# Keeping split weights in memory between the halves of a fused attention and expert kernel, with a reordered prologue and scattered expert rows

## The reference, cut to what matters

```python
xn = _layernorm(x)                                   # 4 x 512 x 512
x = x + attn(xn) + ffn(xn)
...
q, k, v = xn @ Wq.T, xn @ Wk.T, xn @ Wv.T            # 32, 8, 8 heads of 128; rope on q and k
dt = softplus(xn @ Win.T + dt_bias)
g = dt * -exp(A_log_bias)
G = cumsum(g)                                        # within a chunk of 128 tokens
y_intra = (q k^T * causal exp(G_i - G_j)) @ (v * dt)
y_inter = (q * exp(G)) @ state                       # state carried over 4 chunks
y = rmsnorm(y_intra + y_inter) * gnorm_w
attn = (y * silu(xn @ Wg.T)) @ Wo.T
...
scores = softmax(xn @ router_w + router_b) + router_bias
idx = top 2 of 16 experts, out of the best 2 of 4 groups
ffn = sum over the 2 picks of score * expert(xn) + shared_expert(xn)
```

## Time and profile before

| | us |
|---|---|
| median of 3 runs | 2282.23 (2272.57 to 2285.56) |
| the profiled execution | 2264.45 |
| its span in the trace | 2262.7 |
| PE busy | 2073.3 (92% of the span) |
| DVE busy | 1827.1 (81%) |
| ACT busy | 1396.9 (62%) |
| POOL busy | 1012.8 (45%) |

### The profile page before, as it was taken

One profiled execution on the slowest core, in us unless ns is written; L12 is line 12 of the kernel. 1 busy time (PEld: TensorE's weight loads), 2 busy tenths in 40 slices (PEclk: granted clock), 3 DMA queues, 4 the chain that ended last, 5 costly groups with the idle time before them and its releaser, 6 DMA issues.

```text
span 2262.7 us, 34001 instructions
## 1 busy us (share of the span) xinstructions
PE 2073.3 (92%) x9564; PEld 1619.0 (72%) x9564; DVE 1827.1 (81%) x3418; ACT 1396.9 (62%) x2722; POOL 1012.8 (45%) x810
## 2 busy tenths in 40 slices
PE   4699999999999999998899999999999999999990
PEld 2477777777777777776677777777777777767770
DVE  4788888888888888867888888888888888758884
ACT  5366666666666666652566666666666666637870
POOL 1234454545454545444354545454545454432215
PEclk9899999999999999999899999999999999999995
DMA  7212121212121212135121212121212121228667
GB/s 253 72 38 67 37 66 37 65 37 65 37 65 37 65 37 65 37 89 172 38 56 38 65 37 65 37 65 37 65 37 65 37 65 37 75 87 307 212 210 242
DMA packets 150876, 182.26 MB, mean 81 GB/s; under 512 B 13191, under 2 KB 89575, under 8 KB 150782
## 3 DMA queue, kind: packets, MB, share of 16 engines
q1 hardware_dynamic: 135006, 147.08, 22.5%
q0 software_dynamic: 7424, 21.00, 3.0%
q10 hardware_dynamic: 8352, 13.17, 1.6%
HBM read 152.88 MB, written 28.33 MB: 80 GB/s over the span
## 4 chain that ended last, share of the span: by engine, by line
PE 74%; DVE 7%; issue 7%; POOL 6%; ACT 3%; DMA 2%; DVEq 0%; SPq 0%; POOLq 0%; ACTq 0%
PE PJ L1216 10%; PE PJ L1218 10%; PE PJ L1217 10%; PE OU L1216 5%; PE OU L1218 5%; PE OU L1217 5%; PE TR L1360 4%; PE YE L1218 2%; PE YE L1217 2%; PE YE L1216 2%; PE SC L1216 2%; PE CS L1216 2%; PE CS L1217 2%; PE CS L1218 2%; PE YI L1216 2%
## 5 line engine op out<-in xcount | busy, mean ns | idle before, releaser
L444 POOL TENSOR_TENSOR zl<-yb,zh 128x512 fp32r<-128x512 f32 x122 | 162.5, 1332 | 318.4 <-ACT zh L942 318.2
L1216 PE MATMUL OU<-woh,zh 128*128 128x512 f32 x488 | 229.9, 471 | 18.1 <-POOL wol L693 10.2
L1710 DVE TENSOR_TENSOR t<-PJ,cosb 128x512 f32<-128x512 f32 x160 | 110.2, 688 | 168.6 <-PE PJ L1218 120.9
L1216 PE MATMUL PJ<-xnh,wqh 128*128 128x512 f32 x544 | 225.4, 414 | 10.6 <-DVE t L1712 5.8
L958 ACT ACTIVATE qh<-t 128x512 fp32r<-128x512 f32 x128 | 80.9, 632 | 224.0 <-DVE t L1715 224.0
L1218 PE MATMUL PJ<-xnh,wql 128*128 128x512 f32 x544 | 214.4, 394 | 0.0
L1217 PE MATMUL PJ<-xnl,wqh 128*128 128x512 f32 x544 | 214.0, 393 | 0.0
L1216 PE MATMUL PJ<-xnh,wgh 128*128 128x512 f32 x512 | 206.4, 403 | 2.4 <-POOL wgl L693 1.7
L723 POOL TENSOR_TENSOR gm<-gbc,amask 128x512 f32<-128x512 f32 x128 | 166.7, 1303 | 85.2 <-DMA gbc<-decay_exponents 57.4
L1218 PE MATMUL PJ<-xnh,wgl 128*128 128x512 f32 x512 | 201.5, 393 | 0.0
L1217 PE MATMUL PJ<-xnl,wgh 128*128 128x512 f32 x512 | 200.9, 392 | 0.0
(11 more groups left out here) (506 smaller groups left out, 6306.9 us busy)
## 6 DMA issues: line engine op xcount, KB each, us to landing
gbc<-decay_exponents SPq DMA_DIRECT2D x128, 256.0 KB, 4.8
stage<-in_wq SPq DMA_DIRECT2D x72, 256.0 KB
stage<-in_wg SPq DMA_DIRECT2D x64, 256.0 KB
stage<-in_wo SPq DMA_DIRECT2D x64, 256.0 KB
gbc<-in_wm SPq DMA_DIRECT2D x48, 256.0 KB
expert_rows<-rs ACTq DMA_DIRECT2D x48, 256.0 KB
stage<-in_wkv SPq DMA_DIRECT2D x34, 256.0 KB
experts<-in_wm SPq DMA_DIRECT2D x16, 512.0 KB, 6.3
```

The source lines that it names most:

```text
L444: nc.gpsimd.tensor_tensor(lo[:], yb[:, c, :], hi[:].bitcast(F32), ALU.subtract).then_inc(S["zlo"], 1)
L1216: nc.tensor.matmul(out_, a_hi, b_hi, start=first, stop=False)
L1710: v.tensor_tensor(t1[:], PJ[bank][:], cosb[:], ALU.mult)
```

## The change

In half 0, SP also writes both parts of every split piece to memory (`wsp`, shown as `split_weights`). Half 1 loads the two parts straight into their tiles and splits nothing but its first `wq` and the shared expert's weights. The layer norm has smaller groups and six ring buffers, and the decay chain is done by half (256 columns at a time): half 0's before the ropes, half 1's between them. In the middle, the first `wq` is free sooner, and the ranks are made one chunk earlier. In the experts, the map of slots holds beside each token the row where the result belongs, POOL scatters each tile's result there, and at the end SP loads 16 contiguous pieces of 512 KB.

The core of the diff:

```diff
-LN_GROUPS = [slice(0, 2), slice(2, 4), slice(4, 8), slice(8, 16)]
+LN_GROUPS = [slice(0, 2), slice(2, 4), slice(4, 6), slice(6, 8), slice(8, 12), slice(12, 16)]
...
-        xring = [t2[:, 0, :], t2[:, 1, :], gbc[:, 0, :], gbc[:, 1, :]]
+        xring = [t2[:, 0, :], t2[:, 1, :], gbc[:, 0, :], gbc[:, 1, :], st[:], y2[:]]
...
+                    def store_split(k, j):
+                        hold(sp, wsp_out[j % 2], wsp_out_from + 32 * (k * 7 + j // 2))
+                        for i, part_ in enumerate(split_place(j)):
+                            dst = wsp[bass.ds(split_row(k, j), 1), j, i].rearrange("o p n -> (o p) n")
+                            sp.dma_start(dst, plain(part_)).then_inc(wsp_out[j % 2], 16)
+
                     def att_piece(j, src):
                         piece(half, (6 + kv * 14 + j, j % 2), src)
 
+                        if j >= 2:
+                            store_split(kv, j - 2)
...
+                    def load_split(j, back):
+                        for i, part_ in enumerate(split_place(j)):
+                            src = wsp[bass.ds(split_row(kv, j), 1), j, i].rearrange("o p n -> (o p) n")
+                            sp.dma_start(plain(part_), src).then_inc(back, 16)
...
+                    elif half == 1:
+                        gload(0)
+                        gload(1)
+                        at.before("oproj", 4)
...
+                        for j in range(4, 8):
+                            load_split(j, wo_back)
+                        gload(2)
+                        at.wait("proj", 6)
+                        for j in (8, 9):
+                            load_split(j, wkv_back)
+                        gload(3)
+                        for j in range(10, 14):
+                            load_split(j, wq_back)
...
                     def w_lo(j, hi_out, lo_out):
-                        split_lo(half, (6 + kv * 14 + j, j % 2), hi_out, lo_out)
+                        if half == 0:
+                            split_lo(half, (6 + kv * 14 + j, j % 2), hi_out, lo_out)
...
                         def w_hi(j, hi_out):
+                            if half == 1:
+                                return
+                            if not (type(kv) is int and kv == 0):
+                                act.wait_ge(wsp_out[j % 2], wsp_out_from + 32 * (j // 2 - 6) + kv * 224)
                             split_hi(half, (6 + kv * 14 + j, j % 2), hi_out)
...
+            def scatter_rows(i):
+                pool.wait_ge(m_ev, i + 1)
+                g.indirect_dma_start(osd, bass.IndirectOffsetOnAxis(ap=idxt[:, i, 1:2], axis=0), mo[i % 4],
+                                     None).then_inc(mo_out[i % 4], 16)
+
+            for i in range(MT):
+                if i + 4 < MT:
+                    gather_x(i + 4)
+                if i:
+                    scatter_rows(i - 1)
+            scatter_rows(MT - 1)
...
-            act.wait_ge(u_down, NT)
+            act.wait_ge(wq_free, 1)
...
+            results = osd[0:NTA * PICKS * P, :].rearrange("(t p k) n -> t p (k n)", p=P, k=PICKS)
+            for t in range(NTA):
+                sp.dma_start(experts[:, t, :], results[t]).then_inc(pk_in[t // 2][0], 16)
```

More of the change, by code:

```diff
@@ L438, in shared_base, with shared_piece, split_place, split_row @@
         def shared_base(half):
-            return piece_base(half) + 6 + 14 * KV
+            return piece_base(half) + shared_piece(half)
+        def shared_piece(half):
+            return (6 + 14 * KV, 6)[half]
+        def split_place(j):
+            if j < 4:
+                return wgh[:, j, :], wgl[:, j, :]
+            if j < 8:
+                return woh[:, j - 4, :], wol[:, j - 4, :]
+            if j < 10:
+                return wkvflat(wkvh, j - 8), wkvflat(wkvl, j - 8)
+            return wqh[:, j - 10, :], wql[:, j - 10, :]
+        def split_row(kv, j):
+            return kv if j < 8 else kv + 1
         def z_lo(pool, at, c, hi=zh, lo=zl):
@@ L578, in shared_pieces @@
                 for i in range(4):
-                    piece(half, (6 + 14 * KV + i, i % 2), ws1[:, i * PW:(i + 1) * PW])
+                    piece(half, (shared_piece(half) + i, i % 2), ws1[:, i * PW:(i + 1) * PW])
+                    if half == 0 and i < 2:
+                        hold(sp, wsp_out[i], wsp_out_from + 32 * (7 * KV - 1))
+                        for k, part_ in enumerate(split_place(12 + i)):
+                            sp.dma_start(wsp[KV, 12 + i, k], plain(part_)).then_inc(wsp_out[i], 16)
             def shared_bias(half):
@@ L870, in _ @@
             act.wait_ge(const_made, CONSTS)
+            a.activation(klf[:, 511:512], one[:, 0:1], ACT.Sqrt)
             def deviation(r):
@@ L1081, in step @@
                                 silu_gate(c + 1)
+                                if c == 1 and first and half == 0:
+                                    act.wait_ge(g_out, 16 * 8)
                                 exp_g(c + 1)
@@ L1371, in step @@
                             weights(0)
+                        if first and half == 0:
+                            sum_decays(0)
                         at.wait("roperd", 1)
@@ L1379, in step @@
                         ins.then_inc(S["tr"], 1)
+                        if first and half == 0:
+                            turn_decays(0)
                         proj_q(1)
@@ L1389, in step @@
                             proj_q(j)
-                            if j == 2 and first and half == 0:
-                                sum_decays()
                         if b == 1:
@@ L1403, in step @@
                         proj_g(0)
+                        if first and half == 0:
+                            turn_decays(1)
                         at.wait("ropelo", 4)
@@ L1770, in step @@
                             v_rows()
+                            if first:
+                                route_ranks()
                             rope(1, 0)
```

489 lines of the change are left out of this document (277 added, 212 removed).

## The result

| | before | changed |
|---|---|---|
| median of 20 runs, us | 2274.0 | 2263.89 |
| lowest and highest, us | 2260.98, 2285.56 | 2249.14, 2270.24 |
| span of the profiled execution, us | 2262.7 | 2250.4 |

The ratio is 0.9944, with a 95% interval of 0.9924 to 0.9965; the medians differ by 10 us, where 56 were forecast.

A forecast was written before the change was run, and what follows sets the result against it. PE was taken to bound the kernel (busy 2073.3 of 2262.7 us), leaving 189 us of its idle time. Terms −22 (layer norm, step 0) + 2 − 9 − 16 + 0 − 11 = −56 us gave 2226 against the median, range 2196 to 2260.

The forecast's parts named there:

- Half 1, steady: Half 1's later steps: without weight subtractions POOL is 3 us earlier, PE's wait vanishes, 1.0 us over 16 steps: −16 us.
- late loads: Rival: half 1's loads come 2 us late each step, turning the 16 us gain into a loss; 2258 us, chance 0.05.
- The one of the stores: Rival: half 0's stores cost PE about 2.5 us per step, giving back 36 us; 2262 us, chance 0.12.
- the second rival: Half 1 gains nothing because DVE's own ropes set the scores; net −40 us, 2242 us, chance 0.10.
- Half 0: Half 0's steady steps: the added stores cost +2 us over seven groups, bounds −4 and +10.
- Step 0: First step of half 0: shorter waits for the decay chain and scores' inputs, −14.5 us, bounds −7 and −19.
- the layer norm: Start of the kernel: smaller groups and two more ring buffers remove three waits, −7.5 us, between −3 and −16.
- The middle: Between the halves: waits for `wql`, `wgl` and `zl` lose their cause, −9 us, between −4 and −14.
- The experts: Expert loop: tiles stay at 3.71 us with a gather and a scatter each, 0 us, between −4 and +12.
- the end: After the last expert tile: contiguous loads at 309 GB/s, 44 us instead of 55.7, −11 us, between −4 and −15.
- the 2.17 that would decide: Rival: POOL becomes the experts' bound, deciding once a scatter takes 2.17 us; 2293 us at 3.6 us, chance 0.05.

The follow-up runs named there:

- pad_mid: The changed kernel with 24 tiny idle copies in DVE's program between the loops of half 0 and half 1; 2226.66 us, ratio to the kernel before 0.9818.
- split_twice: pad_mid without stores in half 0, half 1 loading the weights and splitting them again as before the change; 2241.36 us, ratio to the kernel before 0.9852.
- before_pad: The kernel before with 38 tiny idle copies in DVE's program at the end of the layer norm; 2263.61 us, ratio to the kernel before 0.9977.
- pairs: The changed kernel with SP storing the parts of two pieces after each second load, so paired loads issue back to back; 2251.41 us, ratio 0.9912.
- gather_end: pad_mid with the end as before the change: ACT stores by slots, POOL's 32 gathers, no scatter; 2254.41 us, ratio to the kernel before 0.9909.

## Why the prediction was wrong, by its own steps

**Half 1, steady: the step that failed.** It said that with the subtractions gone "the wait vanishes" and each step gains 1.0 us, −16 in all. DVE's wait for `ql` did vanish, but two things were left out. The first is the turn of the loop, which the sum put at nothing: +27.1 us, changed kernel against `pad_mid` in steps 18 to 30. Of these PE was idle for 17.7, waiting for the first rope at six turns, and was busy 9.2 longer (725.96 against 716.72) at the lower clock behind it. The rivals had no such case. The one called "late loads" had a time near the measured 2263.89 (2258) by another mechanism: the weights were there when PE asked. The one of the stores was nearer still (2262), also by chance: the stores cost 7 to 11 us where it had 36. The trace of before had the evidence, "issue" time on DVE at each turn of half 0 and none in half 1, and the prediction passed over it, since the change leaves DVE's loop alone. The second is that the gain of 1.0 was too large: `pad_mid`, whose loop is not fetched again, gains 4.3 us in thirteen steps on the kernel before, 0.33 each, and 0.5 each on `split_twice`. PE still waits 1.0 to 1.1 us for the scores in every step of half 1's loop, where it was 1.6 in b = 0 steps and 0.7 in b = 1 steps. The timelines of POOL, DVE and PE show what is left, in the changed kernel:

```profile
1699.94 1.29 POOL L821 TENSOR_TENSOR ql<-t,qh 128x512 fp32r<-128x512 f32 x1 [1.63 <-ACT qh L1067]
1701.20 1.29 POOL L814 TENSOR_TENSOR gm<-gbc,amask 128x512 f32<-128x512 f32 x1
1701.43 1.61 DVE L1864 TENSOR_TENSOR t<-t 128x512 f32<-128x512 f32 x1
1704.79 0.47 PE L1325 MATMUL SC<-qh,kh 128*128 128x512 f32 x1 [1.07 <-issue]
```

and in the kernel before, in the step of the earlier trace rows, whose scores start at 1424.00:

```profile
1420.40 1.29 POOL L723 TENSOR_TENSOR gm<-gbc,amask 128x512 f32<-128x512 f32 x1
1421.35 0.90 DVE L1715 TENSOR_TENSOR t<-t 128x512 f32<-128x512 f32 x1
```

The last operation of DVE's fifth rope, `t<-t`, takes 0.69 us in the first rope of a step (1744.88 in the changed kernel). Beside POOL's `gm` it takes longer, and it ends 0.55 us after `gm` has ended and 1.75 us before the scores start, in both kernels and in all of steps 18 to 30. So the fifth rope does start 1.2 us earlier, but it runs into `gm` sooner and gives 0.7 of that back. "POOL is 3 us earlier" is what failed: `gm` ends only 0.5 to 0.6 us earlier in the step (`pad_mid` against before), as the `ql` ahead of it now waits 1.63 us for ACT's `qh`. That is neither the forecast nor the second rival (DVE's own ropes set the scores), since DVE is held up there by POOL. It is read from the traces; no run here moves `gm`.

**Half 0.** Forecast +2 with a bound of +10; +6.7 over steps 1 to 14, in which the lost fetch of before hides some 4.3 (`before_pad`): without it the change costs 11.0. `split_twice`, which has no stores, takes 2.5 us more than `before_pad` there, for a reason that was not looked for, so the stores made about 8.5. The prediction looked for a late `gbc` load; it was the second `wq` load and ACT's copy of it (`pairs`). It counted the issues and the bytes but not where the loads stand between them.

**Step 0 and the layer norm.** Step 0 was sized well (−11.9 for −14.5). PE now waits 6.75 us for half 1's chain, where about 5 were assumed, and 3.15 us for a rope at 74.86. In PE's timeline of the changed kernel, the layer norm and this wait:

```profile
9.98 1.94 PE L1342 MATMUL PJ<-ident,t 128*128 128x128 f32 x8 [9.98 <-ACT t L970]
15.80 1.12 PE L1342 MATMUL YE<-ident,gbc 128*128 128x128 f32 x4 [2.60 <-ACT gbc L970]
...
85.99 1.22 PE L1381 MATMUL YI<-yb,upper 128*128 128x256 f32 x2 [6.75 <-DVE yb L1772]
```

The layer norm gave 2.6 of 7.5. Its first tile is turned 4 us earlier, at 9.98 instead of 14.02, and PE's idle time fell by 4.2 us in all (24.6 for 28.8), but its busy time rose by 1.7 at a lower clock (0.91 for 0.94). Summing three waits of two engines as if each stood on the path was the error; this is read from the traces and not tested. In nine traces with this prologue the first projection starts at 54.5 to 57.1 us and step 0 takes 64.6 to 67.3 (57.8 and 58.3, 76.5 and 78.0 in two of the kernel before), so both gains are uncertain by 2 to 3 us.

**The middle.** −9.4 for −9, but otherwise made up: steps 16 and 17 gave 12.8, of which 7.9 in step 17 by the loads (`split_twice`), and step 15 with the shared expert lost 3.4. The stores are not the cause of that: `split_twice`, which has none, takes 114.6 us there against 112.0 before, with PE's waits for POOL's `wgl` and `zl` as long as in the changed kernel (2.6 and 2.9 us; 1.9 and 1.4 before). The cause stays open.

**The experts and the end.** The loop stayed near the forecast (2.6 us longer over 48 tiles by `gather_end`); the scatters took 1.26 us each against the 1.08 assumed, far from the 2.17 that would decide. The end was better than forecast, as the loads run at 346 GB/s, not 309: in SP's and DVE's timelines of the changed kernel 16 loads go out in 10 us, and DVE's additions run without a break:

```profile
2215.25 9.82 SPq L743 DMA_DIRECT2D experts<-expert_rows  x16
...
2220.00 5.89 DVE L2225 SCALAR_TENSOR_TENSOR wgh_f<-experts,gates,wgh_f 128x512 f32<-128x512 f32 x8 [9.91 <-DMA experts<-expert_rows]
2231.96 11.69 DVE L2225 SCALAR_TENSOR_TENSOR acc<-experts,gates,acc 128x512 f32<-128x512 f32 x16
```

What remains of the sum without the fetch is `pad_mid`: 2226.66 beside 2268.55 of the kernel before on the same chip, 42 us. That it equals the forecast of 2226 is chance; the terms differ, and the kernel before was measured lower by then.

## What to carry to other kernels

"Issue" time at the head of a loop body, with packets of the instruction queue beside it, was here the loop being fetched again; it can come or go when anything ahead of the loop changes length, so look for it on every engine after each change, and try a dozen or more idle instructions ahead of the loop before judging the change itself (12 and 24 were enough here, 4 were not). Keep bulk loads away from such a turn. A queue in which stores are put between loads delays the second load of a pair: issue the loads first.

## What the runs showed of the hardware that was not expected

- Eight instructions more ahead of a loop (4 and 12 copies) decide whether its 240 instructions are fetched again at each turn: 39 us over six turns, 6.5 us each.
- The same fetch costs DVE 1.6 to 1.9 us with the DMA queues idle, and 3.8 to 4.4 with eight loads of 256 KB beside it; its first packet then starts about 2.4 us later, and takes 0.3 to 0.5 us in both.
- A wait of 2.5 us at the turn costs PE more than itself: the matmuls behind it start 0.43 us apart instead of 0.23 for some 3 us, at a granted clock of 0.50. Over six turns that is 9 us of busy time on top of 18 us of waiting.
- A DVE operation of 0.69 us (`t<-t`, 128x512) takes 1.61 us when POOL's `gm` (1.29 us) has started 0.23 us before it, and ends 0.55 us after `gm` in both kernels.
